# Products of the three older convolution taps on GpSimd, 1024-wide adds on VectorE

## What is computed

```
xz = x @ in_proj_w.T
xi, z = split(xz, 2)
conv[t, c] = sum(conv_w[c, tap] * xi[t + tap - 3, c] for tap in 0..3) + conv_b[c]
xc = silu(conv)
xp = xc @ x_proj_w.T
delta = softplus(xp[0] * dt_w + dt_b)
```

## Time and profile before

| | us |
|---|---|
| median of 3 runs | 7171.37 |
| lowest, highest | 7159.77, 7171.93 |
| profiled execution | 7183.63 |
| its span | 7181.9 |

### The profile page before, as it was taken

How to read it: one execution, slowest core, us unless ns; L and a number is a source line. 1 busy time by engine, 2 the same in 40 slices (tenths; PEclk the granted TensorE clock), 3 DMA queues, 4 the chain that set the end, 5 groups by cost and what they waited for, 6 DMA issues and landing times. The chain is left out here.

```text
span 7181.9 us, 74934 instructions
## 1 busy us (share of the span) xinstructions
PE 6013.7 (84%) x15384; PEld 2658.5 (37%) x15384; DVE 5897.0 (82%) x7250; ACT 4353.1 (61%) x4935; POOL 2905.9 (40%) x2133
## 2 busy tenths in 40 slices
PE   5888888888888888888888888888888888888887
PEld 2333333333333333333333333333333333333333
DVE  4888888888888888888888888888888888888887
ACT  4666665665665656656666566665665665656664
POOL 2444444434434444344443443443434434444342
PEclk8999999999999999999999999999999999999998
DMA  1112112122121221221212212212122121221220
GB/s 56 14 14 14 16 11 17 15 12 17 13 14 15 12 17 15 13 16 12 15 15 12 17 13 13 16 11 17 15 12 17 13 14 15 12 17 15 13 16 9
DMA packets 77669, 109.64 MB, mean 15 GB/s; under 512 B 40336, under 2 KB 40336, under 8 KB 76816
## 3 DMA queue, kind: packets, MB, share of 16 engines
q1 hardware_dynamic: 76816, 100.39, 18.7%
HBM read 42.63 MB, written 16.78 MB: 8 GB/s over the span
## 5 line engine op out<-in xcount | busy, mean ns | idle before, releaser
L651 ACT ACTIVATE decay<-cum,neg_a 128x1024 f32<-128x1024 f32 x1024 | 1139.1, 1112 | 2019.1 <-PE cum L869 2011.8
L427 POOL TENSOR_SCALAR step<-delta,limit 128x1024 f32<-128x1024 f32 x1024 | 1402.3, 1369 | 2117.9 <-PE cum L869 2116.4
L869 PE MATMUL cum<-step,tri_before 128*128 128x512 f32 x4096 | 2114.6, 640 | 126.8 <-issue 123.9
L879 PE MATMUL state<-sources,tri_upto 128*128 128x512 f32 x4096 | 2027.7, 619 | 209.3 <-DVE term L1206 207.6
L437 POOL TENSOR_SCALAR room<-total,limit 128x1024 f32<-128x1024 f32 x1024 | 1318.7, 1288 | 2014.8 <-ACT cum L654 1735.4
L1206 DVE SCALAR_TENSOR_TENSOR term<-state,crow,decay 128x1024 f32<-128x1024 f32 x1024 | 1309.7, 1279 | 870.2 <-PE state L879 576.0
L1216 DVE TENSOR_TENSOR acc<-acc,term 128x1024 f32<-128x1024 f32 x1024 | 1450.7, 1417 | 0.2
L1193 DVE SCALAR_TENSOR_TENSOR sources<-cum,brow,dx 128x1024 f32<-128x1024 f32 x1024 | 1303.6, 1273 | 11.7 <-ACT cum L654 11.7
L869 PEld LDWEIGHTS cum<-step,tri_before 128*128 128x128 f32 x4096 | 804.6, 204 | 1129.5 <-issue 1110.8
L654 ACT ACTIVATE cum<-room,pos_a 128x1024 f32<-128x1024 f32 x1024 | 1147.6, 1121 | 38.5 <-POOL room L437 4.0
L879 PEld LDWEIGHTS state<-sources,tri_upto 128*128 128x128 f32 x4096 | 767.4, 199 | 1073.8 <-issue 1048.6
(11 more groups left out here) (124 smaller groups left out, 4611.6 us busy)
## 6 DMA issues: line engine op xcount, KB each, us to landing
hfirst<-hrows SPq DMA_DIRECT2D x62, 512.0 KB, 20.8
xt<-in_x SPq DMA_DIRECT2D x64, 256.0 KB, 2.7
hrows<-term SPq DMA_DIRECT2D x1024, 4.0 KB, 1.7
xres<-in_x SPq DMA_DIRECT2D x64, 256.0 KB, 2.6
out_x<-xres SPq DMA_DIRECT2D x64, 256.0 KB, 2.0
win<-in_w_in SPq DMA_DIRECT2D x2, 2048.0 KB, 10.3
hrows<-hrows SPq DMA_DIRECT2D x64, 64.0 KB, 2.3
wout<-in_w_out SPq DMA_DIRECT2D x1, 2048.0 KB, 12.8
```

Of the source, the lines that this page charges most:

```text
L427: nc.gpsimd.tensor_scalar(step[s % 2][:, :], delta[t.parity][:, :], limit[:, s:s + 1], 0.0, ALU.min, ALU.max).then_inc(step_ready, 1)
L651: nc.scalar.activation(decay[s % 4][:, :], c, ACT.Exp, scale=neg_a[:, s:s + 1]).then_inc(decay_ready, 1)
L869: last = nc.tensor.matmul(cum[s % 2][:, cols], tri_before[:, :], step[s % 2][:, cols], start=True, stop=True)
L879: last = nc.tensor.matmul(state[:, cols], tri_upto[:, :], source[s % 2][:, cols], start=True, stop=True)
```

## The change

The three older taps are split. GpSimd writes the products of tap 2, 1 and 0 into two buffers `prod0` and `prod1` (tap 2 and tap 0 share the first), eight `tensor_scalar` of 128x128 a tap: those of taps 2 and 1 in its slot 6, those of tap 0 in its slot 7, after VectorE has added tap 2. VectorE adds each product to `conv` with one `tensor_tensor` of 128x1024: tap 2 in slot 7, taps 1 and 0 in slot 8. The newest tap, the halo and all else stay where they are.

```diff
--- before.py
+++ after.py
@@ -49,7 +49,7 @@
 FRONT_ACT = ("xi0", "xi1", "xiT0", "tap3a", "xiT1", "tap3b", "z0", "xcT", "proj", "abs", "exp", "over", "ln", "square", "z1",
              "xc0", "xc1", "ct", "total0", "total1")
 FRONT_PE = ("xi0", "xi1", "xiT0", "xiT1", "z0", "proj", "z1", "xc0", "xc1", "ct", "total0", "total1")
-FRONT_POOL = ("skip",)
+FRONT_POOL = ("tap2", "tap1", "tap0", "skip")
 END_DVE = ("y0", "habs", "hsel", "y1", "gate", "flag", "x2", "stats", "mean_var", "var_eps", "square", "refine", "rstd",
            "xn2", "amax", "scale", "inv", "q_rounded", "q", "scaled", "out")
 END_ACT = ("yT0", "yT1", "log", "guess", "qT")
@@ -154,6 +154,7 @@
         dx = [sb(f"dx{i}", [P, DI]) for i in range(2)]
         total = sb("total", [P, DI])
         ygT = sb("ygT", [P, KI, P])
+        prod = [sb(f"prod{i}", [P, KI, P]) for i in range(2)]
 
 
         step = [sb(f"step{i}", [P, DI]) for i in range(2)]
@@ -413,6 +414,23 @@
                 pool.wait_ge(front_dve, at(FRONT_DVE, t, "poly"))
                 nc.gpsimd.tensor_tensor(acc[t.parity][:, :], xc[:, :], dskip[:, :], ALU.mult).then_inc(front_pool, 1)
 
+            def tap_product(t, tap):
+
+                prev = t.shift(-1)
+                if tap == TAPS - 2:
+                    pool.wait_ge(front_act, at(FRONT_ACT, t, "xiT1"))
+                    pool.wait_ge(front_dve, at(FRONT_DVE, t, "halo_in"))
+                    if prev is not None:
+                        pool.wait_ge(front_dve, at(FRONT_DVE, prev, "tap0"))
+                    stand(pool)
+                if tap == 0:
+                    pool.wait_ge(front_dve, at(FRONT_DVE, t, "tap2"))
+                    stand(pool)
+                for k in range(KI):
+                    last = nc.gpsimd.tensor_scalar(prod[tap % 2][:, k, :], xiT[:, k, tap:tap + P], cw[:, k, tap:tap + 1], 0.0,
+                                                   ALU.mult, ALU.add)
+                last.then_inc(front_pool, 1)
+
             def limit_step(t, s):
                 if s == 0 and t.shift(-1) is None:
                     pool.wait_ge(limit_ready, 2)
@@ -471,6 +489,8 @@
 
             def start():
                 t = Tile(0, 0)
+                for tap in range(TAPS - 2, -1, -1):
+                    tap_product(t, tap)
                 skip(t)
                 for s in range(3):
                     limit_step(t, s)
@@ -490,8 +510,14 @@
                         limit_total(nxt, s + 2 - NS)
                     if s == 0 and prev is not None:
                         finish(prev)
-                    if s == 14 and more:
-                        skip(nxt)
+                    if more:
+                        if s == 6:
+                            tap_product(nxt, 2)
+                            tap_product(nxt, 1)
+                        if s == 7:
+                            tap_product(nxt, 0)
+                        if s == 14:
+                            skip(nxt)
 
             whole(pool, start, body, finish)
 
@@ -1066,11 +1092,8 @@
                     dve.wait_ge(front_dve, at(FRONT_DVE, t, "halo_in"))
                 else:
                     dve.wait_ge(front_dve, at(FRONT_DVE, t, f"tap{tap + 1}"))
-                for k in range(KI):
-                    last = nc.vector.scalar_tensor_tensor(out=conv[:, k, :], in0=xiT[:, k, tap:tap + P],
-                                                          scalar=cw[:, k, tap:tap + 1], in1=conv[:, k, :],
-                                                          op0=ALU.mult, op1=ALU.add)
-                last.then_inc(front_dve, 1)
+                dve.wait_ge(front_pool, at(FRONT_POOL, t, f"tap{tap}"))
+                nc.vector.tensor_tensor(conv[:, :, :], conv[:, :, :], prod[tap % 2][:, :, :], ALU.add).then_inc(front_dve, 1)
                 if tap == 0:
                     nc.vector.tensor_copy(halo[t.parity][:, :, :], xiT[:, :, P:]).then_inc(front_dve, 1)
 
@@ -1290,8 +1313,11 @@
                     if more:
                         if s == 5:
                             front_halo(nxt)
-                        if s in (6, 7, 8):
-                            front_tap(nxt, 8 - s)
+                        if s == 7:
+                            front_tap(nxt, 2)
+                        if s == 8:
+                            front_tap(nxt, 1)
+                            front_tap(nxt, 0)
                         if s == 9:
                             front_rows(nxt)
                             front_dt(nxt)
```

## The result

| | before | after |
|---|---|---|
| median, us (4 runs each) | 7170.26 | 7222.33 |
| lowest, highest | 7159.77, 7171.93 | 7213.54, 7224.28 |
| profiled execution, its span | 7183.6, 7181.9 | 7224.3, 7222.6 |
| mean granted clock | 0.939 | 0.938 |

After takes 1.0073 times as long as before (95% interval 1.0056 to 1.0091): 52 us by the medians, 40.7 us between the two profiled executions. The forecast was 7189 us. The time lies in the stated range (7162 to 7250) and on the side that had the highest chance, but outside the narrower forecast (7180 to 7198), between it and the rival at 7239: the loss is almost three times the 18 us of the sum.

The account below looks back on a forecast made before the run. The prediction took a fixed wait before term 7, set by the broadcast, as the bound, not VectorE's work. Slot 8's adds 12.8, late GpSimd 6 and once-only effects -1 gave +18 us on the 7171 median: 7189, range 7162 to 7250.

Parts of the forecast that it names:

- the rival at 7239: Room 11 and slot 8's adds: each body loses up to one GpSimd instruction, 62 x 1.1 = 68 us; chance 0.18.
- The wall: Before term 7 in slot 8: VectorE waits for term 5's row save, 21.0 to 22.8 us after the broadcast's issue.
- Slot 8, the two adds: Behind the wall, two dependent adds (2.47 us) replace eight taps (2.18): 0.29 us later in 44 bodies, 12.8 us.
- the cover: Slot 8 to the projection: in 18 bodies TensorE at its lower clock was to hide the 0.29 us.
- GpSimd behind the wall: Slot 8's `acc` add held up by late GpSimd reads in 12 tight even bodies, 0.5 us each: 6 us.
- GpSimd is late behind the wall: Same as the rival at 7239: room 11 against slot 8's adds, 62 x 1.1 = 68 us; chance 0.18.
- Its deciding point: The product's price on GpSimd: at 0.3 us a start no body is touched, from about 0.43 us all are.
- a rival of 15 to 25 us on the fast side alone: Luckier placing of TensorE's lower clock: -15 to -25 us, 7150; all faster cases together had chance 0.12.

Follow-up runs that it names:

- products alone: The kernel before, with the 24 products also computed on GpSimd but read by nobody, VectorE keeping its 24 tap instructions; 7202.57 us against 7175.35, ratio 1.0038.
- two zero adds: The kernel before with all 24 taps on VectorE in slots 6 and 7, two dependent adds of zeros in slot 8, no products; 7205.30 us, ratio 1.0041.
- taps ahead of the wall: The kernel before with taps 2 and 1 in slot 6 and tap 0 in slot 7, all on VectorE; 7068.36 us, ratio 0.9846.
- own buffer: The changed kernel with tap 0's products written to `xcT`, so GpSimd does not wait for VectorE's first add; 7217.50 us, ratio 1.0058 to before.
- pure delay: The kernel before with one more VectorE instruction behind the eight of tap 0, on a buffer nobody reads; 7202.64 us against 7171.36, ratio 1.0041.

## Why the prediction was right, and where its sum was wrong

*The wall: right.* Term 7 stands 21.0 to 22.5 us after the broadcast in after, 0.08 to 0.46 us behind the landing of the row of term 5. With the products alone, the two zero adds, the taps ahead of the wall, the own buffer and the pure delay it lies between 21.0 and 22.8 us too; two kernels send the broadcast later and the wall follows; the one that takes it out of slots 5 to 7 gains 2%. The 4.8 us a body that VectorE saves in slots 6 and 7 are worth nothing, as forecast. Where they went was described wrongly in one point: only 149 of the 298 us appear ahead of term 7 (358 instead of 210), and 115 as waits for TensorE's states, 2.0 us a body ahead of term 6, where before had none.

*Slot 8, the two adds: mechanism right, size too small for this kernel.* The term was 44 x 0.29 = 12.8 us. The adds by themselves do cost 0.29 (slot 8 of 6.00 with zero adds); in after it is 0.38 (6.09), the second add starting 1.34 us after the first instead of 1.26. In odd bodies xcT also starts 0.11 us behind the second add instead of 0.03, 0.47 us later than in before. The difference may be the second wait that this add has in after; that was not isolated. The step that failed is the cover: I took 18 bodies out of the sum because TensorE at the lower clock level ended later than xcT there. With a pure delay these bodies pass on 0.22 us. The slack that the earlier trace rows show stands ahead of the projection, but what the end of the tile hangs on is G, and G had moved only 0.13 us in such bodies. In after the odd bodies lose 0.41 us up to G and the 12 even ones that collide with nothing 0.32; taken over 62 bodies that is 23 us in place of 12.8. The zero adds alone make 14 of them (0.23 a body), so the sum of 12.8 was near for the adds themselves, with the wrong number of bodies and too high a price for each; the rest belongs to how the adds stand in this kernel.

*GpSimd behind the wall: right place, wrong count and price.* The product's price was right: eight take 2.80 us, 0.35 from start to start, against 0.32. The term was 12 bodies at 0.5 us. In fact 19 even bodies lose 26 us up to G beyond the 0.32: 10 have the double collision shown above and lose 2.05 us each, 1.5 of them in slot 8, and nine lose 0.6, 0.3 of it in slot 8. I had followed one collision and stopped; the delay that it makes carries the next instruction into another. This is the rival "GpSimd is late behind the wall", with 26 us where it had 68. The zero adds collide with `room` and `step` in six bodies too, without products, but only where VectorE reaches term 7 without idle time, which after never does; there it is GpSimd that is late. Its deciding point was half right: at 0.35 us a start some bodies are touched and not all.

The Trainium skill's rule (SBUF — State Buffer, "Who interferes with whom") holds in the pairs of rows above, to 0.2 us: the later one waits for the whole of the other. Room ends at 1481.59, and the `acc` add that had started beside it ends 1.07 us later. I had applied it as a loss of one short product at a time; the instruction that VectorE met behind the wall is a `room` or `step` of 1.1 us, which the products had only made late.

*Not in the sum.* The change of time behind G, -23 us in the profiled execution, and +9 us from term 12 to the next body, whose cause I did not find. The clock was in the prediction as a rival of 15 to 25 us on the fast side alone; the pure delay shows it on the slow side.

*The medians.* 12.8 + 6 - 1 = 18 us against 49 - 23 + 15 = 41 between the profiled executions. To the 52 between the medians it is 11 more: before's profiled execution is 13 us above its median, after's 2 above its own. By separate kernels the adds cost 31 us and the products 27, together 58 against the 52; that this comes near is no proof, since each has a part from the clock, and the pure delay alone costs 31. That the time lies well inside the range is in part luck: the adds were 10 us too small, late GpSimd 20, and some 15 were missing, and 23 came back behind G; without those the time would have been 7245, at the edge of the range.

The steps that were mis-sized are thus two: the cover of 18 bodies in slot 8 and the price of a late GpSimd behind the wall.

## What to carry to other kernels

Ahead of a wait with a fixed end, find out on which side of it each piece of work stands: taking 4.8 us from the front was worth nothing, moving 2.2 us from behind it to the front was worth 1.5%, and moving the transfer that makes it was worth 2.0%. When work goes from VectorE to GpSimd, count not its busy time but every two-input VectorE instruction that will meet a queue made late, and follow the second collision that the first one causes. The same add can meet GpSimd's ordinary work when it is VectorE that comes late, as the zero adds do in six bodies. Measure landmark to landmark over all bodies, and keep the stretch in which TensorE's clock recovers apart from the rest, or a change of tenths of a microsecond is read with the wrong sign.

## What the runs showed of the hardware that I had not expected

- Two engines that hold each other up settle into taking turns. With the adds behind a late GpSimd queue, `room`, `step` and the adds each take 2.1 us from start to end where they take 1.1 and 1.2 alone, for as long as both have work.
- Another queue does not free small transfers from a large one. The 4 KB saves still landed behind the 512 KB broadcast of 20.8 us when this came from ScalarE's queue (that of term 5 20.9 to 22.7 us after the broadcast's issue). The Trainium skill (DMA: Bandwidth & Descriptors, "Queues, rings and completion order") says that each DMA engine takes turns between its queues a packet at a time, and that a packet typically holds about 9 to 17 descriptors. The trace agrees as far as it goes: the broadcast appears as 128 pieces of 4 KB, 2.3 us each, and 16 of 4 bytes. Spread evenly over 16 engines, an estimate, that is nine for each, few enough for one packet of the page. No run here shows how the pieces are cut into packets.
- At G the same matmuls after the same idle time of 5 us took 2.80 or 3.62 us, by when the granted clock rose from 0.5 to 1.0.
